# Two tiles of A x on TensorE in a Householder tridiagonalisation: the last one as a row, turned

## What is computed

```python
L_norm = d_inv_sqrt[:, None] * L * d_inv_sqrt[None, :]
_, U = jnp.linalg.eigh(L_norm)
agg = jnp.einsum('mn,bnd->bmd', U.T, features)
```

## Time and profile before

| | |
|---|---|
| three runs | 4152.97, 4163.15, 4192.68 us, median 4163.15 |
| profiled execution, span from first to last instruction | 4189.8 us |
| PE busy | 3382.9 us (81%) |
| PE weight loads busy | 2049.1 us (49%) |
| VectorE (DVE) busy | 3298.6 us (79%) |
| ScalarE (ACT) busy | 1532.1 us (37%) |
| mean granted TensorE clock | 0.845 |
| the steps, from the first L486 (58.2) to the last (2189.7) | 2131 us |

### The profile page before, as it was taken

How to read it: one execution, slowest core, us unless ns; L and a number is a source line. 1 busy time by engine, 2 the same in 40 slices (tenths; PEclk the granted TensorE clock), 3 DMA queues, 4 the chain that set the end, 5 groups by cost and what they waited for, 6 DMA issues and landing times. The chain is left out here.

```text
span 4189.8 us, 62612 instructions
## 1 busy us (share of the span) xinstructions
PE 3382.9 (81%) x14639; PEld 2049.1 (49%) x14827; DVE 3298.6 (79%) x21659; ACT 1532.1 (37%) x5534; POOL 55.6 (1%) x71
## 2 busy tenths in 40 slices
PE   5999999999999999988886576554207999998859
PEld 3555555555555665577774322243103444454337
...
PEclk9999999999999899955559887755558999999969
...
GB/s 11 1 1 1 1 1 1 1 1 1 1 1 1 1 2 2 1 1 1 1 1 1 1 1 1 1 1 1 0 20 50 0 0 0 1 0 0 0 6 36
DMA packets 14163, 16.47 MB, mean 4 GB/s; under 512 B 571, under 2 KB 10214, under 8 KB 13798
## 3 DMA queue, kind: packets, MB, share of 16 engines
...
## 5 line engine op out<-in xcount | busy, mean ns | idle before, releaser
L206 PE MATMUL ps<-zero_stream 128*128 128x512 bf16 x2875 | 845.9, 397 | 9.0 <-issue 2.8
L206 PEld LDWEIGHTS ps<-zero_stream 128*128 128x128 bf16 x3045 | 333.6, 126 | 227.7 <-issue 101.7
L304 ACT ACTIVATE refl<-ps,tiny 128x1 f32<-128x1 f32 x511 | 133.5, 261 | 451.4 <-PE ps L244 287.9
L318 ACT ACTIVATE vectors<-WihT,refl 128x4 f32<-128x4 f32 (+2 forms) x383 | 115.0, 300 | 391.9 <-DVE refl L439 387.3
L255 PEld LDWEIGHTS ps<-dot_parts,ones 128*128 128x128 f32 x766 | 133.2, 201 | 203.6 <-DVE dot_parts L433 179.9
L233 PE MATMUL ps<-ident,vectors 128*128 128x128 f32 x1148 | 214.9, 298 | 14.3 <-DVE vectors L486 1.3
L380 DVE CUSTOM_DVE_ANT_0 products<-ps,UT 128x511 f32<-128x511 f32 (+60 forms) x426 | 215.0, 533 | 13.1 <-PE ps L233 12.5
L486 DVE SCALAR_TENSOR_TENSOR vectors<-x_scaled,ps,y_scaled 128x4 f32<-128x4 f32 (+3 forms) x510 | 116.2, 228 | 134.5 <-PE ps L255 89.9
L233 PEld LDWEIGHTS ps<-ident,vectors 128*128 128x128 f32 x1148 | 124.0, 141 | 191.6 <-DVE vectors L486 186.0
L380 DVE CUSTOM_DVE_ANT_0 products<-ps,U 128x499 f32<-128x499 f32 (+57 forms) x402 | 199.2, 524 | 5.1 <-PE ps L233 4.6
L686 ACT ACTIVATE sturm_signs<-sturm_products,sign_bias 128x576 bf16<-128x576 f32 x96 | 74.4, 775 | 350.8 <-DVE products_mark L713 350.8
...
## 6 DMA issues: line engine op xcount, KB each, us to landing
...
x<-in_x_dram SPq DMA_DIRECT2D x4, 0.5 KB
...
```

The costliest lines, as they stand in the source:

```text
L206: nc.tensor.matmul(MA[t][:],still[:,0:P],still[:],start=False,stop=True,skip_group_check=True)
L304: nc.scalar.activation(s[:,u,Y:Y+1],NG[:,0:1] if wide else NG[:,1:2],ACT.Sqrt,bias=tiny[:,0:1]).then_inc(root,1)
```

## The change

Row tiles 2 and 3 of A x both go to TensorE in most steps. Tile 2 comes as before, as a column. Tile 3 comes as a row: x, broadcast, is the stationary operand and A's tile the moving one with 128 columns (`product_as_row`); ScalarE copies one partition of the result to SBUF, and a transpose with one row turns it into a column (`row_turned`). In steps with an update in blocks 0 and 1 only tile 3 is on TensorE, as a row; the first step of a panel in block 0 has it as a column. VectorE keeps two products in block 0 (three where an update runs and in a panel's first step), one or two in block 1 and none in block 2, where x is no longer transposed. Block 2 also takes from block 3 that the dots come with v as the stationary operand and the p column from ScalarE.

The pairs now lie interleaved (u0, w0, u1, w1, ...), so both corrections are one VectorE operation where both factors are in one bank (`by_both`); the sign waits for the pair sums. The norm is a matmul of its own everywhere. x below the diagonal is computed by ScalarE. The pairs are arranged for turning by ScalarE first (`pairs_turned`), and the update has 16 rows where it had 40. In block 3 the selected row is two matmuls. There are fewer zero streams, in another distribution. In the eigenvector stage one addition is added in each of two lists. The core of the diff:

```diff
+def regime(m):
+
+    return min(m//P,3)
+def first_of_panel(m): return m>PANEL and m%PANEL==1
+def row_tile(m):
+
+    if regime(m)==3 or first_of_panel(m) and m<=P+1: return None
+    return NT-1
+def column_tile(m):
+
+    if row_tile(m) is None: return NT-1
+    return None if update_tile(m) and regime(m)<2 else NT-2
 def pe_tiles(m):
 
-    b=m//P
-    if ends_panel(m) and m<=P or m>PANEL and m%PANEL==1 and b<NT-1: return range(0)
-    return range(NT-1,NT)
-
+    tiles=[t for t in (column_tile(m),row_tile(m)) if t is not None]
+    return range(min(tiles),NT)
...
 def streams(m):
...
-    return (1 if b<2 else 0,((6,6,9,6),(5,5,4,4),(4,4,3,5))[b][kind],2)
+    kind=3 if first_of_panel(m) else 2 if ends_panel(m) else 1 if update_tile(m) else 0
+    return (((0,2,2),(0,1,2),(0,1,2),(3,1,2)),((0,2,2),(0,1,2),(0,1,2),(2,1,2)),((2,1,2),(1,1,2),(1,1,2),(2,1,2)),((0,0,0),)*4)[regime(m)][kind]
...
-        def pair_dots(m): return halves(psum[6]) if m<SEP else halves(psum[0]) if m<TAIL else by_kind(psum[1])
...
+        def pair_dots(m): return psum[(7,7,7,1)[regime(m)]][:,0:2+2*SLOTS]
...
+                def row_selected(m, t):
+                    n=2+2*pending(m)[1] if pending(m) else 2
+                    early=m>=TAIL
+                    if early: nc.tensor.matmul(ROWS[:,0:1],pivot(m),XG[:,t,PC_:PC_+1],start=True,stop=True)
+                    lo=2 if early else 0
+                    nc.tensor.matmul(in_pairs(ROWS[:,lo:n]),pivot(m),swapped(XG[:,t,X_+lo:X_+n]),start=True,stop=True).then_inc(sel_ps,1)
+                def product_as_column(m):
+                    b=m//P; r=regime(m); j=column_tile(m)
+                    if j is None: return
+                    o=j-pe_tiles(m)[0]
+                    pe.wait_ge(A_copied,copies_of(version(m)))
+                    if r<2: pe.wait_ge(t2_ready,m)
+                    for t in range(NT-1,b-1,-1):
+                        ins=nc.tensor.matmul(ax(m)[:,o:o+1],A[version(m)%2][:,t,j*P:(j+1)*P],XG[:,t,X_:X_+1],start=t==NT-1,stop=t==b)
+                    if row_tile(m) is None: ins.then_inc(Ax_ps,1)
+                def product_as_row(m):
+                    b=m//P; j=row_tile(m)
+                    if j is None: return
+                    pe.wait_ge(A_copied,copies_of(version(m)))
+                    if m>PANEL: pe.wait_ge(gt_copied,2*((m-1)//PANEL if m<P+PANEL else P//PANEL))
+                    for t in range(b,NT):
+                        ins=nc.tensor.matmul(y_rows(m),XG[:,t,X_:X_+1].broadcast_to([P,P]),A[version(m)%2][:,t,j*P:(j+1)*P],start=t==b,stop=t==NT-1)
+                    ins.then_inc(yr_ps,1)
+                def row_turned(m):
+                    j=row_tile(m)
+                    if j is None: return
+                    o=j-pe_tiles(m)[0]
+                    if regime(m)<2: pe.wait_ge(t2_ready,m)
+                    pe.wait_ge(yr_ready,rows_of_y(m))
+                    nc.tensor.transpose(ax(m)[:,o:o+1],yr[:],ident[0:1,0:1]).then_inc(Ax_ps,1)
...
+                def pair_sums(m):
+                    L=pending(m)
+                    if not L: return
+                    pe.wait_ge(gp_ready,m-1)
+                    nc.tensor.matmul(in_pairs(pair_dots(m)[:,2+2*L[0]:2+2*L[1]]),ones[:],swapped(gp[:,2+2*L[0]:2+2*L[1]]),start=True,stop=True).then_inc(g_ps,1)
...
+                    b=m//P; L=pending(m); tiles=pe_tiles(m); r=regime(m)
                     pe.wait_ge(x_ready,m)
-                    if b<NT-1:
-                        for t in range(b,NT):
-                            ins=nc.tensor.transpose(XR[:,t*P:(t+1)*P],XG[:,t,X_:X_+1].broadcast_to([P,P]),ident[:])
-                        ins.then_inc(xrow_ps,1)
-                        if m>=SEP:
-                            pe.wait_ge(nrm_ready,m); pe.wait_ge(kap_ready,m-1)
-                            nc.tensor.matmul(NG[:,0:1],ones[:],gp[:,0:1],start=True,stop=True).then_inc(s2_ps,1)
+                    if r<3:
+                        if r==2: product_as_row(m)
+                        else:
+                            for t in range(b,NT):
+                                ins=nc.tensor.transpose(XR[:,t*P:(t+1)*P],XG[:,t,X_:X_+1].broadcast_to([P,P]),ident[:])
+                            ins.then_inc(xrow_ps,1)
+                        norm(m)
                         if m>1: pe.wait_ge(ub_ready,m-1); pe.wait_ge(w_ready,m-1)
-                        nc.tensor.matmul(ROWS[:,X_:last_slot(m)],pivot(m),XG[:,b,X_:last_slot(m)],start=True,stop=True).then_inc(sel_ps,1)
+                        row_selected(m,b)
+                        if r<2: product_as_row(m)
+                        pair_sums(m)
+                        if r==2: product_as_column(m); row_turned(m)
                         streamed(m,streams(m)[0])
-                        if m<SEP:
-                            pe.wait_ge(nrm_ready,m)
-                            if m>1: pe.wait_ge(kap_ready,m-1); pe.wait_ge(gp_ready,m-1)
-                            nc.tensor.matmul(NG,ones[:],gp[:],start=True,stop=True).then_inc(s2_ps,1)
+                        if r<2: product_as_column(m); row_turned(m)
+                        if ends_panel(m): transposed(m//PANEL-1)
+                        if update_tile(m): updated(*update_tile(m))
+                        streamed(m,streams(m)[1])
+                        if r<2:
+                            pe.wait_ge(dp_ready,m)
+                            nc.tensor.matmul(dots(m),ones[:],dp[:],start=True,stop=True).then_inc(dot_ps,1)
                         else:
-                            pe.wait_ge(gp_ready,m-1)
-                            nc.tensor.matmul(pair_dots(m),ones[:],halves(gp),start=True,stop=True).then_inc(g_ps,1)
-                        product()
-                        if ends_panel(m): transposed(m//PANEL-1)
-                        early=streams(m)[1]-1 if m>PANEL and m%PANEL==1 else 0
-                        streamed(m,early)
-                        if update_tile(m): updated(*update_tile(m))
-                        streamed(m,streams(m)[1]-early)
-                        pe.wait_ge(dp_ready,m)
-                        nc.tensor.matmul(dots(m),ones[:],dp[:],start=True,stop=True).then_inc(dot_ps,1)
+                            pe.wait_ge(y_ready,m)
+                            for t in range(b,NT):
+                                ins=nc.tensor.matmul(dots(m),V[:,t,m-1:m].broadcast_to([P,P]),XG[:,t,Y_:Y_+2],start=t==b,stop=t==NT-1)
+                            ins.then_inc(dot_ps,1)
                         streamed(m,streams(m)[2])
...
+                        pe.wait_ge(e_ready,m-TAIL+1); pe.wait_ge(kap_ready,m-1)
...
-                        nc.tensor.matmul(ROWS[:,PC_:last_slot(m+1)],pivot(m+1),XG[:,NT-1,PC_:last_slot(m+1)],start=True,stop=True).then_inc(sel_ps,1)
+                        row_selected(m+1,NT-1)
...
+                def pairs_turned(p):
+                    lo=G_+SLOTS*(p%2); sl=slice(panel_block(p),NT)
+                    act.wait_ge(w_ready,PANEL*(p+1)-1); act.wait_ge(ub_ready,PANEL*(p+1)-1)
+                    nc.scalar.copy(turned[:,sl,0:SLOTS],XG[:,sl,lo:lo+SLOTS])
+                    nc.scalar.activation(turned[:,sl,32:32+SLOTS].rearrange("p t (s e) -> p t s e",e=2),XG[:,sl,lo:lo+SLOTS].rearrange("p t (s e) -> p t s e",e=2)[:,:,:,::-1],ACT.Copy,scale=-1.0).then_inc(turned_ready,1)
...
+                    ins=nc.scalar.activation(xm[:,b:b+1],XG[:,b,X_:X_+1],ACT.Copy,scale=below[:,b,i:i+1])
+                    if wide: ins=nc.scalar.copy(xm[:,b+1:NT],XG[:,b+1:NT,X_])
+                    ins.then_inc(xm_ready,1)
+                    if r==0:
                         act.wait_ge(r_ready,m)
-                        nc.scalar.activation(s[:,u,T2:T2+1],NG[:,0:1],ACT.Identity,scale=s[:,u,R:R+1],bias=s[:,u,Y:Y+1]).then_inc(t2_ready,1)
-                        act.wait_ge(h_ready,m); act.wait_ge(t2_ready,m)
+                        nc.scalar.activation(s[:,u,T2:T2+1],norm2(m),ACT.Identity,scale=s[:,u,R:R+1],bias=s[:,u,Y:Y+1]).then_inc(t2_ready,1)
+                    if row_tile(m) is not None:
+                        act.wait_ge(yr_ps,rows_of_y(m))
+                        nc.scalar.copy(yr[:],y_rows(m)[0:1]).then_inc(yr_ready,1)
+                    if r==0:
+                        act.wait_ge(t2_ready,m); act.wait_ge(h_ready,m)
                         nc.scalar.activation(s[:,u,S_:S_+1],s[:,u,T2:T2+1],ACT.Copy,scale=s[:,u,H:H+1]).then_inc(s_ready,1)
-                    if new_rows and SEP<=m<TAIL+PANEL: rows_copied(m//PANEL-1)
+                    if r==2:
+                        act.wait_ge(h_ready,m)
+                        nc.scalar.activation(sh[:,sl],sub[:,sl,i],ACT.Copy,scale=s[:,u,H:H+1]).then_inc(sh_ready,1)
+                    if m>1: reflector_kept(m-1)
...
-                    if not wide:
+                    if r>=2:
                         act.wait_ge(y_ready,m)
-                        nc.scalar.activation(XG[:,sl,PC_],XG[:,sl,C_],ACT.Identity,scale=s[:,u,S_:S_+1],bias=XG[:,NT-1,Y_:Y_+1]).then_inc(pc_ready,1)
```

(39 more changed lines are left out.)

215 lines of the change are left out of this document (95 added, 120 removed).

## The result

The change makes the kernel slower: 4778.59 us (median of four runs, 4754.16 to 4786.0) against 4164.54, a ratio of 1.146 (95% interval 1.141 to 1.151). I had forecast 4395 us, with 4540 as the upper end. The direction was right; the loss, 614 us, is more than twice the 232 I had worked out.

The account below looks back on a forecast made before the run. A step was taken to be as long as VectorE's serial list plus its waits for TensorE. Full-clock terms -32+6-6+51 = +19 us and +213 us for the clock, together +232, made 4395 us; 8-in-10 range 4095 to 4540.

Parts of the forecast that it names:

- What a step costs at either level: Blocks 0 to 2: low-clock steps of 7.4, 6.4 and 5.8 us, on average 2.4 us above the full-clock step.
- block 0: First 128 columns, full clock: steps of about 4.66 to 5.15 us, a gain of 32 us over 16 panels.
- How many steps are low: Blocks 0 to 2: 120 steps at the low clock cost 288 us, less 75 lost already: +213 us.
- the 75 of before: Blocks 0 to 2 of the kernel before: the low clock already takes some 75 us.
- clock mostly low: Rival for blocks 0 to 2: half of the steps at the low clock, +400 us, 4563 us; chance 0.13.
- Block 1 at the full clock: Second 128 columns: 4.26 us a step against 4.13, as the wait eats the saved product; +6 us.
- Block 2 at the full clock: Third 128 columns: next x at 3.45 us against 3.52, no gain in update steps; -6 us.
- Block 3: Last 128 columns, half clock: two more selection passes ahead of the norm add 0.41 us 127 times; +51 us.
- As before: Rival for blocks 0 to 2: row passes replace the streams and the clock stays as it was; 4210 us, chance 0.18.
- clock stays up: Rival for blocks 0 to 2: row products keep the clock up, 75 us come back; 4107 us, chance 0.18.
- The cheap selection: Rival for block 3: split selection nearly free at 0.11 us a pass, 24 us less, clock as before; 4186 us, chance 0.06.

Follow-up runs that it names:

- a_plus2: The changed kernel with two more zero streams in almost every step of blocks 0 to 2: 4471 us, ratio 1.071.
- a_order: The changed kernel with three waits taken back, zero streams redistributed and TensorE's list reordered, with pair sums inside the row product: 4320 us, ratio 1.033.
- a_waits: The changed kernel with block 3's row selected in one matmul, its norm awaiting kappa only at the first step, block 2's p column by VectorE: 4674 us.

## Why the prediction was wrong, point by point

**What a step costs at either level: right, in the blocks it was worked out for.** At the full clock, block 0: forecast 4.66 for two tiles, 4.7, 5.0 and 5.15; measured medians 4.68 to 4.72, 4.75, 5.15 and, in a_plus2, 5.12 to 5.15 (two tiles, a panel's end, its first step, a step with an update). Adding up the full-clock steps of each place in the panel (with those of a_plus2 where the changed kernel has none) and taking off the same sum of the kernel before, block 0 would gain 34 us; I had 32. At half clock: forecast 7.4, 6.4 and 5.8 us; measured 7.46, 6.60 and 6.09 on average, 6.53 and 5.89 in plain steps of blocks 1 and 2. Over the full-clock steps that is 2.0 to 2.7 us; I had 2.4.

**How many steps are low: the step that failed.** I wrote "three steps in each of 16 panels of block 0 and three in 12 panels each of blocks 1 and 2, so 120 steps". The time at the lower level makes 430/7.46=58 such steps in block 0, close to 48; but 656/6.60=99 in block 1 and 574/6.09=94 in block 2, where I had 36 each. Together 251 steps at 2.4 us are 602 us, less the 75 of before: 527 instead of 213. This one term carries 314 of the 382 us by which the sum fell short. (With the distance that each block showed, 2.66, 2.03 and 2.27 us, the 251 steps are 568 us, so 2.4 was a little high.) I had taken the length of a fall from the kernel before ("falls before lasted two to seven steps"), where five to twelve streams a step stood ready to bring the clock back. I had seen that there would be fewer to come back by, and gave it no number. In block 1 the seven steps m=137 to 143 are only part of a fall: from m=131 to 143 every step is wholly at the lower level. That the missing streams are what lets a fall last is shown by a_plus2, where two more a step take block 1 from 656 to 48 us at the lower level. The rival "clock mostly low" had the right mechanism with 190 steps and 4563 us; I gave it 0.13, and it too stopped short.

**Block 1 at the full clock: under-sized.** Forecast 4.26, measured 4.35 to 4.41 (4.30 to 4.37 in a_plus2); with the steps that carry an update or start a panel, some 29 us instead of 6. The list I had written was right up to the pair sums (sign 2.23 us after x), but sign, shift, merged product and reduction came one behind the other, and a_order showed that the turned row stands 0.26 us behind them as the next wait.

**Block 2 at the full clock: wrong, by a wait I had not followed.** Forecast 3.45, measured 3.74; 32 us more instead of 6 less. I had taken the p column off VectorE and not asked what stands behind it on ScalarE. a_waits settled it: with that alone undone, 3.43.

**Block 3: right, with a second wait hidden behind the first.** Forecast 3.4 to 3.5 us and +51 us; measured 3.51 and +61. The two passes move the norm by 0.43 us, as worked out, which is 55 us in 127 steps; with the 8 us that stay when everything is undone that is 63, near the 61. But undoing the passes alone brought only 33 us back, because the wait for kappa, which stands in the diff and which I did not price, takes over at 0.50 us. Both together give 53. The Trainium skill (TensorE: Matmul & The Clock Gate, LDWEIGHTS) made this term 27 us with 107 ns for a load; at half clock the passes start 0.21 us apart in the trace after as before, and the measurement decides against it.

**The rivals.** "As before" and "clock stays up" are out: 0.58 to 0.72 where they need 0.9 or more. The cheap selection is out by block 3. The sum with the measured terms is -34+29+32+61+527=615, and 581 with the 568 us for the low steps, against 591 between the spans.
